# Two-layer transformer on one core: SyncE loads slot numbers four at a time, and GpSimd's sums between sends are left out

## The chip, the cores and the metric

The kernel runs on one core of one Trainium2 chip. The metric is the time of one execution on the device in microseconds (us). A core has five engines with instruction streams of their own: TensorE (PE in the profile; its weight loads are PEld), VectorE (DVE), ScalarE (ACT), GpSimd (POOL) and SyncE (SP, its queue SPq). They meet only through semaphores. In this kernel SyncE computes nothing: it waits, reads small numbers into registers and issues direct DMAs. GpSimd issues the indirect ones, and does elementwise work.

## The reference, cut to what matters

Eight batches of 512 tokens with 128 features go through two layers. Each layer adds an attention and then a mixture of experts to the tokens:

```
x = x + attention0(layernorm(x))      # 16 heads of 8, 4 key/value heads, causal
x = x + moe0(layernorm(x))            # 8 experts, the best one per token: silu(x w1a) * (x w1g) @ w2, times its probability
x = x + attention1(layernorm(x))      # latent keys and values, rotary positions, causal
x = x + moe1(layernorm(x))            # 8 experts, the best two per token: relu(x w1 + b1) @ w2 + b2, times the probabilities
```

Which expert a token goes to is known only when the gate has been computed on the chip. The change touches the two mixtures alone.

## The kernel before, in words

**Slots.** The tokens of a group of batches are sorted by expert. GpSimd scatters each tile of 128 tokens with an indirect DMA to rows of a DRAM tensor `sorted_in` (step `scatter`, line 1090), so that each block of 128 rows there holds tokens of one expert. Such a block is a slot. Layer 0 has two groups (batches 0 to 3 and 4 to 7) with 46 slots in all; layer 1 has four groups (batches 0 to 3; 4 and 5; 6; 7) with 78 slots. In the three last groups of layer 1, which share a half (a group is then called streaming), the rows of a slot lie at a place that is known only at run time.

**What is done for a slot of layer 1.** SyncE fetches the first weights of its expert into a ring of six buffers (`fetch_w1`, lines 913 to 933, 322 KB), and its rows, four slots per step (`fetch`, lines 945 to 967). TensorE turns the rows (`turn_rows`, L1299), multiplies by the first weights (`first`, L1317, 8 matmuls a slot) and by the second (`second`, L1327, 8 matmuls). ScalarE does the relu between them (L1476). VectorE adds the bias out of the ring's buffer (`second`, L1507, `w<-psum,w_now`), once a slot; with it the ring's buffer and the psum bank are free again. GpSimd then sends the 128 rows back to their tokens' places with an indirect DMA (`send`, L1098). At the end SyncE takes each half back (`take_back`, L988), VectorE adds it to X with the gates (L1541), and SyncE stores X.

**Numbers in registers.** The expert of a slot is a whole number in the table `expert_of`, the place of a streaming slot's rows one in `tile_at`. For each slot SyncE reads the number into a register with `value_load` (L916 for the expert, L962 for the place).
**The order.** Every engine's order of steps is written out by hand as a string of letters (`ORDERS`, one letter a step, from which `Plan.read_orders` makes the steps). Each engine follows its string strictly, so a step that waits holds up all that stands behind it on its engine. On SyncE, in the streaming groups, one `fetch` step (B) alternates with some three or four `fetch_w1` steps (D). `fetch_w1` waits, after its load, until VectorE or TensorE has freed the ring's buffer.

**Pauses.** `read_orders` marks a scatter, a combine (layer 0's gather back, L1108) or a send as one with a pause when two such steps stand directly before it (`MOST_IN_A_ROW` = 2). Before such a step GpSimd adds four columns of constants (`pause`, lines 1019 to 1023, `route_small<-consts`), with a wait for the pause before. By the order string there are 62 pauses: 20 before scatters, 2 before combines and 40 before sends.

Of the kernel before, what the change touches and what calls it, by code (L numbers as in the profile page):

```python
# [20 lines left out]
EXPERTS = 8  # L21
# [116 lines left out]
REGION_TILES = REGION // P  # L138
# [141 lines left out]
XT_KINDS = ("turn", "turn_ctx")  # L280
INDIRECT = ("scatter", "combine", "send")
MOST_IN_A_ROW = 2

def slot_before(layer, g, x, n):
# [109 lines left out]
class Plan:  # L395
# [53 lines left out]
    def read_orders(self):  # L449

        number = dict.fromkeys(SORTED, 0)
        for engine, letters in ORDERS.items():
            queues = {}
            for s in self.steps:
                if (s.kind not in SORTED or apart(s)) and takes_part(s, engine):
                    queues.setdefault(LETTERS[s.kind], []).append(s)
                elif SORTED.get(s.kind) == engine and takes_part(s, engine):
                    queues.setdefault(LETTERS[variant(s)], []).append(s)
            for kind, first_on in SORTED.items():
                if engine != first_on and kind != "add":  # L460
                    queues[LETTERS[kind]] = [s for s in self.orders[first_on] if s.kind == kind and takes_part(s, engine)]
            queues = {letter: iter(steps) for letter, steps in queues.items()}
            in_a_row = 0
            for letter in letters:
                s = next(queues[letter])
                self.orders[engine].append(s)
                if SORTED.get(s.kind) == engine:
                    s.n = number[s.kind]
                    number[s.kind] += 1
                if s.kind in XT_KINDS and engine == "pe":  # L470
                    n = len(self.users["xt"])
                    s.slot, s.turn = n % 3, n // 3
                    self.users["xt"].append(s)
                if s.kind == "stats" and engine == "dve":
                    s.slot = s.n % 2
                if engine == "pool":
                    s.pause = s.kind in INDIRECT and in_a_row == MOST_IN_A_ROW
                    in_a_row = (1 if s.pause else in_a_row + 1) if s.kind in INDIRECT else 0

    def take_banks(self):  # L480
# [42 lines left out]
def two_layers(nc, d):  # L523
    with ExitStack() as ctx:
# [278 lines left out]
        def _(sp):  # L803
            def load_batch(b):
                sp.dma_start(X[:, QT * b:QT * b + QT, :], d["x"].rearrange("b (t p) d -> b p t d", p=P)[b]).then_inc(x_loaded[b], DMA)

            load_batch(0)
            sp.dma_start(consts[:, :], d["consts"]).then_inc(consts_loaded, DMA)
            sp.dma_start(scratch[:, 0:MASK_COLS], d["masks"]).then_inc(consts_loaded, DMA)
# [18 lines left out]
            for s in plan.order("sp"):  # L828
# [83 lines left out]
                elif s.kind == "fetch_w1":  # L912
                    if s.x == 0:
                        sp.wait_ge(experts_known, ALL_GROUPS.index((s.layer, s.b)) + 1)
                    j = first_slot(s.layer, s.b) + s.x
                    e = sp.value_load(expert_of[half_of(s.layer, s.b)][0:1, j:j + 1], min_val=0, max_val=EXPERTS - 1)  # L916
                    if s.turn:

                        old = slot_before(s.layer, s.b, s.x, W1_RING[s.layer])
# [24 lines left out]
                elif s.kind == "fetch":  # L944
# [9 lines left out]
                    if streams(s.layer, s.b):  # L954
# [2 lines left out]
                        if s.x == 0 and is_final(s.layer, s.b):  # L957
                            sp.wait_ge(tails_set, EXPERTS * DMA)
                        tiles = sorted_in[s.layer][half_of(s.layer, s.b)].rearrange("(n p) d -> n p d", p=P)
                        for t in range(n):  # L960
                            j = first_slot(s.layer, s.b) + 4 * s.x + t
                            at = sp.value_load(tile_at[0:1, j:j + 1], min_val=0, max_val=EXPERTS * REGION_TILES + SPARE - 1)  # L962
                            sp.dma_start(rows_in[s.slot][:, t * ROW:(t + 1) * ROW],  # L963
                                         tiles[bass.ds(at, 1), :, :].rearrange("a p d -> p (a d)")).then_inc(fetched[s.slot], DMA)
                        continue
# [888 lines left out]
```

## Time and profile before

| | |
|---|---|
| runs | 1048.46, 1060.53, 1063.93 us |
| median | 1060.53 us |
| profiled execution: from its first to its last instruction (the page gives no other time of it) | 1059.9 us |
| TensorE busy, mean granted clock | 902.2 us (85%), 0.92 |
| VectorE, ScalarE, GpSimd busy | 667.9, 610.0, 534.5 us |
| moved by DMA | 141.20 MB, mean 133 GB/s |

How to read it: busy shares are averages over stages that have different limits. To about 210 us there is the attention of layer 0 alone; from there on the experts of a group run beside the attention of the batches behind it. The last attention ends near 840 us, and what is left to the end is the experts of layer 1 alone. Waiting, register and branch instructions don't count as busy, so SyncE has no busy share; its instructions are seen in the views of a line and in the chain of waits.

### The profile page before, as it was taken

To read this page: it belongs to the slowest core of one execution; us is meant where nothing else is said; L and a number is where in the kernel's file an instruction comes from. 1 tells how busy PE (TensorE), PEld (TensorE's weight loads), DVE (VectorE), ACT (ScalarE), POOL (GpSimd) and SP (SyncE) were. 2 spreads that over 40 slices of the span, in tenths; PEclk is the share of its full clock that TensorE was granted. 3 is DMA by queue.
4 is the path that set the end of the run, shared out by engine and by line. 5 is a ranking of instruction groups with operands and counts; after the bars stand their busy time and mean duration, and the time that the engine had idled before them with its cause. 6 is when DMAs were issued, how large, how long until landed. Compare 5 with 4: busy or idle time off the path is not lost.

```text
span 1059.9 us, 25406 instructions
## 1 busy us (share of the span) xinstructions
PE 902.2 (85%) x8968; PEld 600.8 (57%) x8968; DVE 667.9 (63%) x1379; ACT 610.0 (58%) x1173; POOL 534.5 (50%) x809
## 2 busy tenths in 40 slices
PE   4699999879998999889998999978998776399791
PEld 2344554436995445349974454534447766388781
DVE  1889897857457888855669987997861351011116
ACT  3168897825445786734346867856784343155541
POOL 3144454562015776752137855676865633744442
PEclk9999999879999899789999989998988888699996
DMA  5635523353755253519844273345023445357577
GB/s 145 138 85 161 152 70 88 83 162 108 216 170 125 92 144 86 128 43 302 234 133 81 84 160 93 95 116 149 28 61 90 143 133 152 99 164 217 164 211 226
DMA packets 137317, 141.20 MB, mean 133 GB/s; under 512 B 35564, under 2 KB 113452, under 8 KB 137100
## 3 DMA queue, kind: packets, MB, share of 16 engines
q1 hardware_dynamic: 130604, 126.04, 43.7%
q0 software_dynamic: 6592, 13.55, 4.1%
q8 instruction: 76, 1.25, 0.5%
q14 instruction: 45, 0.37, 0.1%
HBM read 98.73 MB, written 44.36 MB: 135 GB/s over the span
## 4 chain that ended last, share of the span: by engine, by line
PE 30%; DVE 6%; another core or an unknown queue 5%; issue 5%; SPq 4%; ACT 3%; DMA 2%; POOL 0%; DVEq 0%; ACTq 0%; POOLq 0%
PE psum L1317 8%; PE psum L1327 7%; PE psum L1248 4%; DVE neg_max L1510 2%; PE psum L1204 2%; PE psum L1230 2%; SPq L963 1%; ACT scratch L1439 1%; SPq L962 1%; PE psum L1210 1%; PE psum L1274 1%; SPq L933 1%; SPq L916 1%; PE psum L1283 1%
## 5 line engine op out<-in xcount | busy, mean ns | idle before, releaser
L1510 DVE TENSOR_REDUCE neg_max<-psum 128x2 f32<-128x768 f32 (+3 forms) x352 | 380.7, 1120 | 73.2 <-PE psum L1210 52.2
L1439 ACT ACTIVATE scratch<-psum 128x1024 f32<-128x1024 f32 x320 | 316.7, 1024 | 97.2 <-PE psum L1230 84.3
L1079 POOL TENSOR_SCALAR_AFFINE_SELECT scratch<-scratch 128x512 f32<-128x512 f32 x256 | 159.0, 642 | 150.8 <-ACT scratch L1439 149.6
L1317 PE MATMUL psum<-rows_t,w_now 128*128 128x128 f32 x1360 | 177.6, 284 | 5.3 <-issue 2.2
L1248 PE MATMUL psum<-scratch,values 128*32 128x512 f32 (+3 forms) x2048 | 173.4, 460 | 1.3 <-POOL scratch L1079 0.3
L1317 PEld LDWEIGHTS psum<-rows_t,w_now 128*128 128x128 f32 x1360 | 165.6, 198 | 13.8 <-issue 8.8
L1327 PE MATMUL psum<-w,hidden_t 128*128 x992 | 140.7, 292 | 36.4 <-ACT hidden_t L1476 15.5
L1204 PE MATMUL psum<-k_stack,q_stack 52*128 52x128 bf16 (+3 forms) x1024 | 136.2, 326 | 25.7 <-DVE neg_max L1510 10.2
L1476 ACT ACTIVATE hidden_t<-psum,w_now 128x128 f32<-128x128 f32 x312 | 88.7, 372 | 115.0 <-remote 39.6
L1327 PEld LDWEIGHTS psum<-w,hidden_t 128*128 128x128 f32 x992 | 128.0, 204 | 43.4 <-issue 43.2
L1230 PE MATMUL psum<-q_stack,k_stack 55*128 55x512 bf16 (+3 forms) x1024 | 124.9, 316 | 14.5 <-DVE neg_max L1510 5.6
L1090 POOL DMA_INDIRECT sorted_in<-xn_half,rows_of x96 | 94.4, 984 | 50.7 <-DVE xn_half L1532 28.2
L1507 DVE TENSOR_TENSOR w<-psum,w_now 128x128 f32<-128x128 f32 x78 | 22.6, 291 | 154.5 <-PE psum L1327 94.6
L1098 POOL DMA_INDIRECT returned<-w,goes_to x78 | 76.8, 984 | 81.0 <-DVE w L1507 50.7
L1204 PEld LDWEIGHTS psum<-k_stack,q_stack 52*128 52x128 bf16 x1024 | 44.0, 98 | 107.2 <-issue 45.4
L1210 PE MATMUL psum<-masks_bf 64*128 64x64 bf16 (+2 forms) x1408 | 94.6, 213 | 2.0 <-issue 2.0
L1248 PEld LDWEIGHTS psum<-scratch,values 128*32 128x32 f32 x2048 | 55.6, 112 | 65.1 <-issue 44.7
L1210 PEld LDWEIGHTS psum<-masks_bf 64*128 64x128 bf16 x1408 | 71.9, 102 | 34.1 <-issue 8.8
L1230 PEld LDWEIGHTS psum<-q_stack,k_stack 55*128 55x128 bf16 x1024 | 37.0, 96 | 75.8 <-issue 36.1
L1764 DVE SCALAR_TENSOR_TENSOR hidden_t<-w,psum 128x512 f32<-128x512 f32 x46 | 31.6, 687 | 59.1 <-PE psum L1327 33.8
L1061 POOL TENSOR_TENSOR rot<-rot 128x512 f32<-128x512 f32 x16 | 20.4, 1273 | 54.6 <-DVE rot L1507 54.5
L1069 POOL TENSOR_TENSOR max_parts<-max_rest,max_parts 32x128 bf16<-32x128 f32 x32 | 13.6, 424 | 59.7 <-ACT max_parts L1335 59.4
(141 smaller groups left out, 1027.5 us busy)
## 6 DMA issues: line engine op xcount, KB each, us to landing
w_now<-in_w SPq DMA_DIRECT2D x78, 322.0 KB
w_now<-in_w SPq DMA_DIRECT2D x46, 512.0 KB
q_stack<-q_parts SPq DMA_DIRECT2D x64, 192.0 KB
q_parts<-q_parts SPq DMA_DIRECT2D x16, 384.0 KB, 3.2
k_stack<-k_parts SPq DMA_DIRECT2D x32, 192.0 KB
q_parts<-q_parts SPq DMA_DIRECT2D x16, 256.0 KB, 3.0
w<-in_w SPq DMA_DIRECT2D x16, 256.0 KB, 4.5
scratch<-returned SPq DMA_DIRECT2D x16, 256.0 KB, 3.6
```

What stands on the lines that cost most here:

```text
L1079: pool.affine_select(out=diag, in_=diag, compare_op=ALU.is_ge, fill=0.0, base=0, pattern=[[0, 4], [1, P]], channel_multiplier=-1).then_inc ...
L1090: pool.indirect_dma_start(sorted_in[s.layer][half_of(s.layer, g)][:, :], bass.IndirectOffsetOnAxis(ap=row_of(s.layer, g, t, k), axis=0), x ...
L1098: pool.indirect_dma_start(returned[h][:, :], bass.IndirectOffsetOnAxis(ap=goes_to[h][:, j:j + 1], axis=0), kept[slot], None).then_inc(sent ...
L1204: pe.matmul(out[:, j * width:(j + 1) * width], q_stack[i][rows, pair, t * P:(t + 1) * P], k_stack[i][rows, k_of(layer, pair), 0:width], st ...
L1210: ins = pe.matmul(blocks, ident_of[half, :], mask[half, :].unsqueeze(1).to_broadcast([P // 2, n, P // 2]), start=False, stop=(first > widt ...
L1230: ins = pe.matmul(bank[u.bank + k][:, off:off + SEQ - j * P], k_stack[i][rows, k_of(layer, pair), j * P:(j + 1) * P], q_stack[i][rows, pai ...
L1248: ins = pe.matmul(bank[u.bank][CW * c:CW * c + CW, j * P:SEQ], values[batch_of(s) % 3][:, j, col:col + CW], p[:, c % 2, off:off + SEQ - j ...
L1317: ins = pe.matmul(bank[v.bank][:, c * P:(c + 1) * P], w1_now[layer][w.slot][:, n * FFN + c * P:n * FFN + (c + 1) * P], rows)
L1327: ins = pe.matmul(bank[u.bank][:, 0:P], hidden_t[h.slot][:, k * P:(k + 1) * P], w2[layer][:, bass.ds(e, 1), k * DIM:(k + 1) * DIM].rearran ...
L1439: act.activation(expd[s.slot], psum[:, u.bank:u.bank + 2, :], ACT.Exp, scale=SCALE).then_inc(read[u.bank], 1)
L1476: ins = act.activation(hidden_t[s.slot][:, c * P:(c + 1) * P], bank[u.bank][:, c * P:(c + 1) * P], ACT.Relu, bias=w[:, FFN + c:FFN + c + 1])
L1510: return dve.tensor_reduce(out=out, in_=in_, axis=AX, op=op, negate=negate)
```

## The change

SyncE reads the numbers of up to four slots at once with `values_at`, without the comparison of bounds: `fetch_w1` does so at each fourth slot of a group and takes one number from the list at each step; `fetch` reads its up to four places before it issues its up to four DMAs. TensorE's loads (L1309) and those of the tails (L941) stay as they are. In `read_orders` a send gets no pause any more. A send still counts as a step in a row, and `>=` stands for `==`, so that a scatter behind two or more sends gets one: by the order string 23 pauses are left, 21 before scatters and 2 before combines.

```diff
+LOADED = 4
...
                 if engine == "pool":
-                    s.pause = s.kind in INDIRECT and in_a_row == MOST_IN_A_ROW
+                    s.pause = s.kind in INDIRECT and s.kind != "send" and in_a_row >= MOST_IN_A_ROW
                     in_a_row = (1 if s.pause else in_a_row + 1) if s.kind in INDIRECT else 0
...
+            def values_at(table, first, n, high):
+
+                found = nc.values_load_multi_w_load_instructions(
+                    table[0:1, first:first + n], engines=[mybir.EngineType.SP], min_val=0, max_val=high,
+                    skip_runtime_bounds_check_because="the table is made on the chip of counts that cannot leave these bounds")
+                return list(found[1])
...
                 elif s.kind == "fetch_w1":
                     if s.x == 0:
                         sp.wait_ge(experts_known, ALL_GROUPS.index((s.layer, s.b)) + 1)
-                    j = first_slot(s.layer, s.b) + s.x
-                    e = sp.value_load(expert_of[half_of(s.layer, s.b)][0:1, j:j + 1], min_val=0, max_val=EXPERTS - 1)
+                    if s.x % LOADED == 0:
+                        experts = values_at(expert_of[half_of(s.layer, s.b)], first_slot(s.layer, s.b) + s.x,
+                                            min(LOADED, SLOTS[s.layer][s.b] - s.x), EXPERTS - 1)
+                    e = experts.pop(0)
...
-                        for t in range(n):
-                            j = first_slot(s.layer, s.b) + 4 * s.x + t
-                            at = sp.value_load(tile_at[0:1, j:j + 1], min_val=0, max_val=EXPERTS * REGION_TILES + SPARE - 1)
+                        found = values_at(tile_at, first_slot(s.layer, s.b) + 4 * s.x, n, EXPERTS * REGION_TILES + SPARE - 1)
+                        for t, at in enumerate(found):
                             sp.dma_start(rows_in[s.slot][:, t * ROW:(t + 1) * ROW],
                                          tiles[bass.ds(at, 1), :, :].rearrange("a p d -> p (a d)")).then_inc(fetched[s.slot], DMA)
```

## Rows read from the trace of the kernel before

**Rows 1.** The page: busy time by engine; the chain that ended last, by engine.
```profile
PE 902.2 (85%) x8968; PEld 600.8 (57%) x8968; DVE 667.9 (63%) x1379; ACT 610.0 (58%) x1173; POOL 534.5 (50%) x809
...
PE 30%; DVE 6%; another core or an unknown queue 5%; issue 5%; SPq 4%; ACT 3%; DMA 2%; POOL 0%; DVEq 0%; ACTq 0%; POOLq 0%
```

**Rows 2.** The chain of waits from 944 to 1006 us: shares by line.
```profile
by line: issue 24.8%; SPq L963 20.5%; SPq L962 18.3%; SPq L933 15.0%; SPq L916 14.7%; DMA w_now<-in_w 5.9%; DMA rows_in<-sorted_in 2.9%; SPq L928 0.6%; SPq L953 0.1%; SPq L956 0.1%; SPq L958 0.0%
```

**Rows 3.** Busy by stretch: us, PE, PEld, DVE, ACT, POOL, clock, DMA, GB/s.
```profile
944.00:1006.00 62.00, 54.70 (x435) 50.06 (x434) 7.68 (x31) 33.44 (x114) 28.26 (x39) 1.00 0.64 185
1006.00:1035.00 29.00, 25.92 (x205) 25.07 (x206) 4.12 (x15) 14.09 (x49) 13.03 (x18) 0.94 0.72 211
```

**Rows 4.** Timeline of VectorE: start, us, line, operation, [idle before]; three bias additions.
```profile
945.15 0.29 DVE L1507 TENSOR_TENSOR w<-psum,w_now 128x128 f32<-128x128 f32 x1 [1.49 <-PE psum L1327]
...
1007.86 0.29 DVE L1507 TENSOR_TENSOR w<-psum,w_now 128x128 f32<-128x128 f32 x1
...
1039.22 0.29 DVE L1507 TENSOR_TENSOR w<-psum,w_now 128x128 f32<-128x128 f32 x1 [0.67 <-PE psum L1327]
```

**Rows 5.** Groups by line, 944 to 1006, then 1007.8 to 1039.3: bias additions.
```profile
L1507 DVE TENSOR_TENSOR w<-psum,w_now 128x128 f32<-128x128 f32 x25 | 7.1, 291 | 28.1 <-PE psum L1327 23.8 <-issue 4.3
...
L1507 DVE TENSOR_TENSOR w<-psum,w_now 128x128 f32<-128x128 f32 x16 | 4.7, 292 | 24.2 <-PE psum L1327 16.8 <-issue 7.5
```

**Rows 6.** SyncE's waits (total, times, longest): 944 to 1006; 1007.8 to 1039.3; whole kernel.
```profile
SPq L928 <- DMA w_now<-in_w: 1.7, 2, 1.3
...
SPq L933 <- DVE w L1507: 5.5, 4, 2.2
...
SPq L933 <- PE psum L1317: 33.6, 27, 3.2
```

**Rows 7.** Loads of line 962, 944 to 1006: count, ns min/median/max.
```profile
L962 SPq TENSOR_LOAD <-tile_at x28: 3/268/422, 944.3 to 1005.2; - x28
```

**Rows 8.** The chain from 1004 to 1006: start, us, what; one place and its DMA.
```profile
1004.11 0.27 SPq L962
...
1004.41 0.15 SPq L962
...
1004.68 0.04 SPq L963
...
1004.83 0.34 SPq L963
...
1005.21 0.28 SPq L962
```

**Rows 9.** Timeline of GpSimd, 904 to 924: sends, and a pause (L1023).
```profile
904.98 1.00 POOL L1098 DMA_INDIRECT returned<-w,goes_to  x1 [0.16 <-issue]
906.28 0.96 POOL L1098 DMA_INDIRECT returned<-w,goes_to  x1 [0.30 <-issue]
907.27 0.21 POOL L1023 TENSOR_TENSOR route_small<-consts 128x4 f32<-128x4 f32 x1
907.64 1.00 POOL L1098 DMA_INDIRECT returned<-w,goes_to  x1 [0.16 <-issue]
...
922.26 0.96 POOL L1098 DMA_INDIRECT returned<-w,goes_to  x1 [0.30 <-issue]
```

**Rows 10.** The whole kernel's pauses (L1023): count, ns min/median/max, first and last.
```profile
L1023 POOL TENSOR_TENSOR route_small<-consts x62: 207/208/224, 219.6 to 1039.4; 128x4 f32<-128x4 f32 x62
```

**Rows 11.** The chain of waits, 900 to 926: its pieces with no releaser found.
```profile
906.50 6.72 another core or an unknown queue
913.26 12.02 another core or an unknown queue
```

**Rows 12.** Timeline, 913 to 926: VectorE, TensorE and ScalarE around the longest piece.
```profile
913.25 0.29 DVE L1507 TENSOR_TENSOR w<-psum,w_now 128x128 f32<-128x128 f32 x1 [12.55 <-remote]
...
913.78 2.07 PE L1327 MATMUL psum<-w,hidden_t 128*128 x8 [8.51 <-DVE w L1507]
...
925.30 0.89 ACT L1476 ACTIVATE hidden_t<-psum,w_now 128x128 f32<-128x128 f32 x3 [18.80 <-remote]
```

## The prediction, made before the changed kernel ran

> **What bounds the kernel now.** I read the page first. TensorE is busy for 85% of the span and leads the chain that ended last, but SyncE's queue holds 4% of that chain, with part of the 5% called issue, and another 5% has no releaser that the profile can name [rows 1]. So neither of the two engines that the change touches bounds the kernel as a whole; the question is where their 4% and 5% lie. The chain of waits in the stretch from 944 to 1006 us answers the first: the four lines of SyncE hold 20.5 + 18.3 + 15.0 + 14.7 = 68.5% of it, "issue" (here the gaps between SyncE's own instructions) 24.8%, and no matmul stands in it at all [rows 2]. For 62 us SyncE is the bound. TensorE is busy there for 54.7 of 62 us at full clock [rows 3], which looks like a bound too; but a matmul's modelled end covers gaps shorter than it, so I go by the pace instead.
>
> The pace is read off VectorE's bias additions, one a slot. From 945.15 to 1007.86 there are 25 [rows 4, 5], so 62.71 / 25 = 2.51 us a slot. From 1007.86 to 1039.22 there are 16 with both ends, so 15 steps, 31.36 / 15 = 2.09 us a slot, at a mean clock of only 0.94 [rows 3 to 5]. What differs is SyncE: in the first stretch it waits for nobody but 1.7 us for weights, in the second it waits 5.5 us for VectorE to free the ring [rows 6]. There TensorE and what hangs on it set the pace; before, SyncE did.
>
> The views of GpSimd answer the second question. While it sends indirect DMAs back to back, signals between other engines come late: between the bias addition at 913.25 and the relu at 925.30 the chain has a piece of 12.02 us without a releaser, before it one of 6.72 us [rows 11], and VectorE sat for 12.55 us, ScalarE for 18.80 us [rows 12]. Both pieces lie in a row of sends that begins at 904.98 and whose last starts at 922.26 [rows 9].
>
> **SyncE, step by step.** A streaming slot costs SyncE two numbers and two DMAs. For one place the load begins at 1004.11, the comparison at 1004.41, the address at 1004.68, the DMA at 1004.83, and the next load at 1005.21 [rows 8]. So a number with its DMA takes 1.10 us: load and gap 0.30, comparison, assertion and their gaps 0.27, address 0.15, DMA and gap 0.38. A slot takes 2.20 us of SyncE; the 2.51 measured have waits and slower issues on top, 0.31.
>
> The change removes the comparison at both: 2 x 0.27 = 0.54 us a slot. How long one load of four numbers takes no row shows. From below it is one single load, 0.268 us [rows 7]; from above four of them in a row with their gaps, 4 x 0.30 = 1.20 us. The slot then costs SyncE 2.20 - 0.54 = 1.66 us at the upper end and 1.66 - 2 x 0.30 x 3/4 = 1.21 us at the lower. I take the upper end, since only single loads are in the rows. With the 0.31 of waits it is 1.97, under 2.09 at either end: SyncE stops being the bound, and TensorE's pace is late next. The gain is 25 x (2.51 - 2.09) = 10.5 us at most. I take 9: two or three slots of it go while the ring of six fills, and the transfers get denser, as the DMA share of 0.72 against 0.64 shows at the faster pace [rows 3].
>
> The Trainium skill (Runtime: NRT & Kernel Launch, Instruction fetch mechanics) says that a bulk TENSOR_LOAD costs some 200 ns for each register. This speaks against half the change; an estimate by it is 0.8 us for four numbers, in which case the slot would cost SyncE 1.46 us with 0.31 on top, and the sum would stay, since TensorE's pace still ends it. No run so far shows such a load.
>
> A step that is moved: at a `fetch` the first row DMA leaves later, up to 1.20 + 0.15 instead of 0.57 + 0.15 us behind the step's start; its fourth starts at 1.20 + 3 x 0.53 + 0.15 = 2.94 instead of 3 x 1.10 + 0.72 = 4.02. TensorE and VectorE wait for all four, so this is a gain. The first `fetch_w1` of a group leaves up to 0.63 us later, and its second at 1.88 against 1.82, the others earlier. In six groups that is at most 6 x 0.63 = 3.8 us, and less wherever the rows are still under way; at the lower end it is a gain of 0.27 each. I take nothing.
>
> In layer 0, and where a `fetch_w1` waits for the ring, the load stands ahead of the wait and is hidden by it: SyncE waits 33.6 us in 27 pieces for TensorE there [rows 6]. If that cover went, each number would give 0.27 back. Nothing.
>
> **GpSimd, step by step.** 40 pauses go and one is added: net 39 of 62, 0.208 us each [rows 10]. In a row of sends the pause costs less than its length: from 906.28 to 907.64 with it is 1.36 us, from 904.98 to 906.28 without is 1.30 [rows 9]. That is 0.06 us for each; 8 lie in the long row, 0.5 us, which stands on the chain. Elsewhere GpSimd waits for VectorE and the pause runs in that wait. I take 0.4. What three or more indirect DMAs without a sum cost, or do to the late signals, no row shows: from above no gain over the sum's 0.06, from below no row. So it is bounded by the rivals.
>
> **Sum.** The profiled execution spans 1059.9 us, 0.6 under the median of 1060.53, in runs that spread over 15 us. 1059.9 - 9 - 0.4 = 1050.5; against the median 1051. What follows the last bias addition, 1059.9 - 1039.2 = 20.7 us, moves as it is.
>
> **Rivals.**
>
> *Another wait takes SyncE's place.* At a denser issue the weights land late, or the upper end of the load plus slow issues beside the sends keeps SyncE near 2.3 us a slot: 25 x 0.2 = 5 us or less, and where the comparison stayed in after all, 0 to 2. Around 1057. For it: SyncE already waited for weights twice in the stretch [rows 6]. Against: the later stretch holds 2.09 with 211 GB/s against 185 [rows 3].
>
> *Slower: the pause is what lets the signals through.* Place: the sends in a row from 904.98 on. Without pauses GpSimd's sequencer may run further ahead, and the signals that came in the middle of the row, such as VectorE's at 913.25, come only behind the last send. The eight matmuls at 913.78 and what they released (some 5 us of TensorE's work, [rows 12]) would then move behind 923; if the late signals of the shorter rows double as well, 6.72 + 12.02 = 18.7 us more at the worst. I price it at 16: 1059.9 - 9.4 + 16 = 1066.5. It decides from 9.4 us on, 0.24 us for each pause that is gone. For it: the late signals stand only in such rows. Against: pauses at 907.27 and each 2.7 us after did not end them [rows 9, 11].
>
> The Trainium skill (Perfetto Trace Analysis, DMA Instruction — SWDGE (GPSIMD)) bears on it: GpSimd's sequencer pushes such a DMA into a wait queue and goes on at once to the next. The trace of before can't show how far it runs; by that rule only the pause's own wait holds it back.
>
> *The pause holds the signals up.* If sums with their own semaphore are part of what makes them late, half of 18.7 us and of like pieces before it comes back, some 12: 1059.9 - 9.4 - 12 = 1038.5. For it: 8 pauses stand in the very stretch. Against: an unpaused pair is just as tight.
>
> **How the numbers follow.** Forecast 0.58, its own range 1044 to 1057; another wait 0.15 (1057); pause missing, slower 0.14 (1067); pause harmful 0.13 (1038). A measurement of this kernel can tell about 2% from no change, 21 us: under 1039 or over 1082. Under 1039 lies half of the last case and a little of the forecast, as medians of a few runs move by some us: 0.14. Over 1082 lies only the far end of the slower case: 0.04. The rest, 0.82, is within 2%. The range 1040 to 1065 leaves out about half of either outer case.
>
> **What would show it.** In the chain from some 935 us on, SyncE's lines should be gone and matmuls stand there; bias additions should follow each other by about 2.1 us; SyncE should wait for VectorE at L933 all the way. L916 and L962 should show no comparison any more, and one load for four numbers or one for each. Sends in a row should start every 1.30 us, with 23 sums left. The prediction is wrong if the pace stays over 2.3 us, or if the pieces without a releaser behind 850 us change by more than 5 us in either direction.

## The result, and the profile after

In the first comparison, 20 runs of each kernel side by side, the changed kernel took 1049.34 us (median; 1038.79 to 1054.51) and the kernel before 1057.37 us (1048.46 to 1072.52): a ratio of 0.9913, with an interval of 0.9892 to 0.9934. The forecast was 1051 us in a range of 1040 to 1065. The profiled execution spans 1047.5 us against 1059.9.

The page of the changed kernel: busy time by engine, and further down the chain that ended last, by engine; they answer to [rows 1].

```profile
PE 895.6 (86%) x8968; PEld 596.9 (57%) x8968; DVE 671.3 (64%) x1379; ACT 609.9 (58%) x1173; POOL 524.8 (50%) x770
...
PE 35%; DVE 6%; another core or an unknown queue 6%; issue 3%; ACT 2%; DMA 1%; POOL 0%; SPq 0%; DVEq 0%; ACTq 0%; POOLq 0%
```

SyncE's 4% are gone from the chain and TensorE took them. The pieces without a releaser are still there. The same is to be seen in the stretch of [rows 2]: the chain of waits of the changed kernel from 944 to 998 us, shares by line (L1326 and L1336 are the matmuls of a slot, L1317 and L1327 before).

```profile
by line: PE psum L1336 49.0%; PE psum L1326 38.7%; PE psum L1308 5.1%; issue 3.3%; DVE w L1516 1.7%; ACT hidden_t L1485 1.4%; ACT rows_t L1344 0.9%; ACTq L1483 0.0%
```

Busy time by stretch of the changed kernel, with the columns of [rows 3]: us, PE, PEld, DVE, ACT, POOL, clock, DMA share, GB/s.

```profile
944.00:998.00 54.00, 51.25 (x424) 48.24 (x423) 8.02 (x32) 31.04 (x107) 24.02 (x25) 1.00 0.76 221
998.00:1027.00 29.00, 27.57 (x230) 26.32 (x230) 5.41 (x21) 16.77 (x58) 14.07 (x15) 1.00 0.72 226
```

VectorE's bias additions of the same three slots as in [rows 4], from the timeline of the changed kernel.

```profile
943.47 0.29 DVE L1516 TENSOR_TENSOR w<-psum,w_now 128x128 f32<-128x128 f32 x1 [1.50 <-PE psum L1336]
...
997.72 0.29 DVE L1516 TENSOR_TENSOR w<-psum,w_now 128x128 f32<-128x128 f32 x1 [0.49 <-PE psum L1336]
...
1026.90 0.29 DVE L1516 TENSOR_TENSOR w<-psum,w_now 128x128 f32<-128x128 f32 x1 [0.23 <-issue]
```

These three rows carry the whole account. Up to the first of them the changed kernel is 945.15 - 943.47 = 1.7 us ahead. The 25 slots after it take 54.25 us where they took 62.71, so 8.5 us, or 2.17 against 2.51 us a slot. The next 15 take 29.18 instead of 31.36, 2.2 us. What follows the last is 20.7 us before and 20.6 after. 1.7 + 8.5 + 2.2 + 0.1 = 12.4 us, the difference of the two spans.

Most of the 2.2 us is TensorE's clock. The stretch of the kernel before ends with TensorE idle for 3.10 us behind SyncE's late rows. After one more group of eight matmuls at full speed, the granted clock falls: it is 0.57 of full over the next 3.9 us, the lower of its two levels for most of them. Here are TensorE's rows there, then busy time in those 3.9 us and in all 15 slots (columns of [rows 3]):

```profile
1008.40 1.15 PE L1327 MATMUL psum<-w,hidden_t 128*128 x8 [3.10 <-DVE w L1507]
1009.72 1.76 PE L1317 MATMUL psum<-rows_t,w_now 128*128 128x128 f32 x8 [0.16 <-issue]
...
1009.72:1013.65 3.93, 3.93 (x21) 3.93 (x22) 0.46 (x2) 1.14 (x4) 1.68 (x3) 0.57 0.75 230
...
1007.86:1039.22 31.36, 29.24 (x230) 28.01 (x230) 5.68 (x22) 15.63 (x54) 16.08 (x22) 0.95 0.75 228
```

The same of the changed kernel, where TensorE had waited only 0.30 us:

```profile
998.26 1.15 PE L1336 MATMUL psum<-w,hidden_t 128*128 x8 [0.30 <-DVE w L1516]
999.58 1.13 PE L1326 MATMUL psum<-rows_t,w_now 128*128 128x128 f32 x8 [0.16 <-issue]
...
997.72:1026.90 29.18, 27.81 (x233) 26.37 (x231) 5.59 (x20) 16.89 (x59) 13.97 (x15) 1.00 0.73 228
```

In the chains of waits the matmuls of L1317, L1327 and L1299 at this place take 1.76, 1.71 and 0.63 us before and 1.13, 0.89 and 0.44 after: 1.6 of the 2.2 us. The other 0.5 us are spread over the twelve slots behind them.

SyncE's waits in the changed kernel (in total, times, longest), 944 to 998, then 998 to 1027: they answer to [rows 6].

```profile
SPq L938 <- DMA w_now<-in_w: 3.3, 2, 3.0
SPq L943 <- DVE w L1516: 3.0, 4, 1.0
...
SPq L943 <- DVE w L1516: 9.9, 6, 2.4
```

SyncE now has time to wait for VectorE in both stretches. Its loads in the changed kernel from 944 to 998 (count, ns min/median/max, first and last start), which stand in the place of [rows 7]; the first table feeds the weights, the second the rows.

```profile
L810 SPq TENSOR_LOAD <-expert_of x8: 285/872/933, 945.6 to 995.5; - x8
L810 SPq TENSOR_LOAD <-tile_at x6: 863/888/931, 950.2 to 991.1; - x6
```

Fourteen loads instead of one a number, and no comparison behind them. A load of four is 0.87 to 0.89 us in the middle, 0.22 a number, where a single one takes 0.268 and 0.30 with its gap; so little is gained by taking them together. The shortest, 0.285 us, is a load of one number: the group of batches 4 and 5 has nine slots, and 4 + 4 + 1 are loaded. The last loads of two other groups have two and three numbers and take 0.467 and 0.677 us:

```profile
L810 SPq TENSOR_LOAD <-expert_of x1: 285/285/285, 953.2 to 953.2; - x1
L810 SPq TENSOR_LOAD <-tile_at x1: 467/467/467, 998.6 to 998.6; - x1
L810 SPq TENSOR_LOAD <-expert_of x1: 677/677/677, 925.0 to 925.0; - x1
L810 SPq TENSOR_LOAD <-expert_of x3: 299/304/308, 872.1 to 897.1; - x3
```

The last line stays unexplained: these three, ahead of the stretch, are loads of four too and took 0.30 us.

GpSimd in the changed kernel: the timeline of the long row of sends, then all pauses. They answer to [rows 9] and [rows 10].

```profile
903.90 0.96 POOL L1107 DMA_INDIRECT returned<-w,goes_to  x1 [0.31 <-issue]
905.17 0.96 POOL L1107 DMA_INDIRECT returned<-w,goes_to  x1 [0.30 <-issue]
...
920.35 0.96 POOL L1107 DMA_INDIRECT returned<-w,goes_to  x1 [0.31 <-issue]
```

```profile
L1032 POOL TENSOR_TENSOR route_small<-consts x23: 207/208/221, 217.9 to 901.0; 128x4 f32<-128x4 f32 x23
```

A send follows the one before it every (920.35 - 903.90) / 13 = 1.265 us; with a pause after each pair it was (922.26 - 904.98) / 13 = 1.33 [rows 9]. The pieces without a releaser in the chain of the changed kernel from 850 to 926 us, which answer to [rows 11]:

```profile
856.43 4.40 another core or an unknown queue
...
874.88 10.90 another core or an unknown queue
899.71 8.92 another core or an unknown queue
908.94 15.23 another core or an unknown queue
```

They are about as long as before. Two of them, 8.92 + 15.23 = 24.2 us, lie in the long row, where the kernel before had 6.72 + 12.02 and one of 2.66 just ahead, 21.4.

### The profile page after: what moved, and what is told of

It is laid out like the page before. It is cut to its first block, busy times and chain, and to the rows that moved or that the text cites. A ratio compares the mean times of both kernels' runs of the same rounds, so it can differ in the third digit from the quotient of the medians.

```text
span 1047.5 us, 24922 instructions
## 1 busy us (share of the span) xinstructions
PE 895.6 (86%) x8968; PEld 596.9 (57%) x8968; DVE 671.3 (64%) x1379; ACT 609.9 (58%) x1173; POOL 524.8 (50%) x770
## 4 chain that ended last, share of the span: by engine, by line
PE 35%; DVE 6%; another core or an unknown queue 6%; issue 3%; ACT 2%; DMA 1%; POOL 0%; SPq 0%; DVEq 0%; ACTq 0%; POOLq 0%
PE psum L1326 10%; PE psum L1336 9%; PE psum L1257 5%; PE psum L1239 3%; PE psum L1213 3%; DVE neg_max L1519 2%; PE psum L1219 1%; PE psum L1283 1%; PE psum L1308 1%; ACT scratch L1448 1%; PE psum L1292 1%; PE psum L1175 1%; PE psum L1267 1%; DVE X L1550 1%
## 5 line engine op out<-in xcount | busy, mean ns | idle before, releaser
L1326 PE MATMUL psum<-rows_t,w_now 128*128 128x128 f32 x1360 | 176.6, 283 | 4.8 <-issue 3.0
L1326 PEld LDWEIGHTS psum<-rows_t,w_now 128*128 128x128 f32 x1360 | 164.9, 197 | 13.3 <-issue 11.1
L1336 PE MATMUL psum<-w,hidden_t 128*128 x992 | 138.9, 289 | 33.5 <-DVE w L1516 13.0
L1336 PEld LDWEIGHTS psum<-w,hidden_t 128*128 128x128 f32 x992 | 126.3, 202 | 40.4 <-issue 40.3
```

The costliest lines, as they stand in the source:

```text
L1326: ins = pe.matmul(bank[v.bank][:, c * P:(c + 1) * P], w1_now[layer][w.slot][:, n * FFN + c * P:n * FFN + (c + 1) * P], rows)
L1336: ins = pe.matmul(bank[u.bank][:, 0:P], hidden_t[h.slot][:, k * P:(k + 1) * P], w2[layer][:, bass.ds(e, 1), k * DIM:(k + 1) * DIM].rearran ...
```

## The experiments

Every kernel was timed in turn with the kernel before; kernels of one batch share a chip and the runs of the kernel before, and each ratio is to those. The batches ran on chips 11, 5, 2 and 13, in this order; the number of the chip of the first comparison is not on record.

**The parts taken apart.** The first batch of four holds each half of the change alone, and SyncE's half in two ways: loads without comparison, but one number each; and loads of four numbers with their comparisons.

`pause_only` has GpSimd's half: the changed rule for pauses, SyncE as before.

```diff
-                    s.pause = s.kind in INDIRECT and in_a_row == MOST_IN_A_ROW
+                    s.pause = s.kind in INDIRECT and s.kind != "send" and in_a_row >= MOST_IN_A_ROW
```

> GpSimd's part alone: no pause before a send, SyncE as before. Theory A (SyncE's shorter work gives the gain): at most 0.5 us below the kernel before plus what the faster row of sends gives back, ratio 0.998 to 1.000; bias additions between 945 and 1008 us still 2.5 us a slot. Theory B (the pauses gave the gain): ratio 0.992. Theory C (pauses let late signals through): slower, ratio over 1.003. Sends in a row start every 1.27 us instead of 1.33 under all three.

`sp_only` has SyncE's half: the changed kernel with the old rule for pauses.

```diff
-                    s.pause = s.kind in INDIRECT and s.kind != "send" and in_a_row >= MOST_IN_A_ROW
+                    s.pause = s.kind in INDIRECT and in_a_row == MOST_IN_A_ROW
```

> SyncE's part alone: four numbers a load, no comparison, pauses as before. Theory A: ratio 0.991 to 0.993, bias additions 2.1 to 2.2 us a slot in the long stretch. Theory B: ratio 0.998 to 1.000. Theory C: faster than the whole change.

`single_unchecked` is `sp_only` with one number a load, still without comparison.

```diff
-LOADED = 4
+LOADED = 1
...
-                        found = values_at(tile_at, first_slot(s.layer, s.b) + 4 * s.x, n, EXPERTS * REGION_TILES + SPARE - 1)
-                        for t, at in enumerate(found):
+                        for t in range(n):
+                            at = values_at(tile_at, first_slot(s.layer, s.b) + 4 * s.x + t, 1, EXPERTS * REGION_TILES + SPARE - 1)[0]
```

> One number a load as before, but no comparison of bounds; pauses as before. By the rows, a slot costs SyncE 1.66 us and 0.3 of waits, below TensorE's 2.1. Theory A1 (once SyncE is under TensorE's pace more is worth nothing): the same as SyncE's part alone, ratio 0.991 to 0.993. Theory A2 (the load of four matters too): half of it, ratio 0.995 to 0.997.

`bulk_checked` is `sp_only` with the comparison of each of the four numbers put back.

```diff
-                    table[0:1, first:first + n], engines=[mybir.EngineType.SP], min_val=0, max_val=high,
-                    skip_runtime_bounds_check_because="the table is made on the chip of counts that cannot leave these bounds")
+                    table[0:1, first:first + n], engines=[mybir.EngineType.SP], min_val=0, max_val=high)
```

> Four numbers a load, each still compared with its bounds; pauses as before. The load of four was 0.87 us in the streaming groups after the change, 0.22 a number against 0.30, so a slot costs SyncE 2.20 - 0.16 = 2.04 us and 0.3 of waits, 2.35 against 2.51. Theory A1: a third to a half of the gain, 25 x 0.16 = 4 us, ratio 0.996. If the load of four is what counts: ratio 0.992.

| kernel | median us | ratio | interval | the 25 slots of the profiled execution |
|---|---|---|---|---|
| before | 1057.43 | 1 | | 62.71 us [rows 4] |
| pause_only | 1055.44 | 0.9983 | 0.9954 to 1.0011 | 61.88 |
| sp_only | 1047.02 | 0.9903 | 0.9867 to 0.9939 | 54.37 |
| single_unchecked | 1047.2 | 0.9895 | 0.9860 to 0.9930 | 54.55 |
| bulk_checked | 1056.63 | 0.9991 | 0.9966 to 1.0017 | 63.11 |

The last column is the time from the bias addition at the start of the stretch to the one 25 slots later. Without comparison the kernel gains, whether it loads four numbers or one; with it it gains nothing, though it loads four. Busy time from 944 to 998 us, in the columns of [rows 3], of `sp_only`, `single_unchecked`, `bulk_checked` and `pause_only`:

```profile
944.00:998.00 54.00, 51.02 (x424) 48.20 (x424) 8.06 (x31) 30.28 (x103) 26.66 (x37) 1.00 0.75 220
```

```profile
944.00:998.00 54.00, 50.90 (x422) 47.99 (x421) 8.27 (x32) 31.14 (x107) 26.21 (x37) 1.00 0.75 215
```

```profile
944.00:998.00 54.00, 47.55 (x383) 43.93 (x382) 7.28 (x28) 28.29 (x97) 25.83 (x36) 1.00 0.62 185
```

```profile
944.00:998.00 54.00, 47.98 (x388) 44.33 (x386) 7.29 (x28) 28.28 (x95) 21.72 (x23) 1.00 0.68 197
```

The two without comparison put 424 and 422 matmuls into the same 54 us, the two with it 383 and 388. What a load of four with comparison costs is seen in `bulk_checked`'s instructions of line 810 from 944 to 1006 us (ns min/median/max):

```profile
L810 SPq FUSED_REGOPS  x53: 5/147/348, 944.6 to 1003.8; - x53
L810 SPq SEQ_ASSERT  x53: 3/18/18, 944.8 to 1003.9; - x53
L810 SPq TENSOR_LOAD <-tile_at x7: 868/951/1054, 943.7 to 1001.9; - x7
```

Each of the 53 numbers has its comparison and its assertion again, whichever load it came with. The expectation of a third to a half of the gain (a load of four saves 0.08 us a number, 4 us in 25 slots) missed: nothing came. In the chain of `bulk_checked` from 944 to 1006 us SyncE shares the time with the weights' transfers and some matmuls, where before it stood nearly alone [rows 2]:

```profile
by line: SPq L810 21.6%; DMA w_now<-in_w 19.8%; issue 19.7%; SPq L971 13.3%; SPq L942 8.4%; PE psum L1335 8.3%; PE psum L1325 8.1%; DMA rows_in<-sorted_in 3.0%; DVE w L1515 0.5%; SPq L937 0.2%; SPq L962 0.1%; SPq L967 0.0%; SPq L965 0.0%
```

So what SyncE saves in its loads did not reach TensorE: waits for transfers took its place in the chain. Why they do, no run took apart.

The last 15 slots divide the five kernels in the same way. They take 31.31 us in `bulk_checked` and 30.70 in `pause_only`, at a mean granted clock of 0.95 and 0.94, and 29.50 in `sp_only` and 29.66 in `single_unchecked`, at 1.00. TensorE sat idle for 2.41 and 3.01 us ahead of the dip in the first two, and for 0.30 and 0.32 us at this place in the others.

**The late signals.** The next four ask what the pieces without a releaser hang on. `sends_moved` leaves the changed kernel's instructions as they are and only moves letters in GpSimd's written order: eleven sends of layer 1's first group (8) go in between the last two portions of scatters, three into the sixes and eight more into the sevens, so that the one long row is split and the sends keep up with the slots.

```diff
-        "ppp4pb44p44bp4m44pp4ppp44m44ppppppp55pppbpp55558855558b5888858855888558866666666777787777888888888888888888888888999999999++++++++"
+        "ppp4pb44p44bp4m44pp4ppp44m44ppppppp55pppbpp55558855558b5888858855888558866668886666777788888888877778888888888888999999999++++++++"
```

> The whole change, and GpSimd's order altered at one place: of the sends that stood in one row behind the last scatters of layer 1, three go ahead of four scatters that wait till 873 us, and eight more ahead of the four that wait till 898 us. Theory L (signals between engines come late as long as GpSimd issues indirect DMAs back to back): the row from 899 to 921 us shrinks to some 9 us, the bias addition of slot 29 comes near 910 us instead of 924, some 10 us are won, ratio to the kernel before 0.980 to 0.986. Rival (the late signals come from something else at that place, or only move): within 0.3% of the whole change, 0.989 to 0.993.

It took 1038.17 us, 0.9802 (0.9742 to 0.9862), as expected if the row is what counts (0.980 to 0.986). Its chain has these pieces without a releaser from 850 to 926 us:

```profile
872.43 13.22 another core or an unknown queue
897.44 4.30 another core or an unknown queue
902.91 3.83 another core or an unknown queue
```

That is 21.4 us, where the changed kernel has 4.40 + 10.90 + 8.92 + 15.23 = 39.5. The work is the same; so the pieces go with the length and the place of GpSimd's row. The changed kernel itself wasn't timed on this chip; `no_pause`, below, stands in for it.

`no_pause` takes the last 23 pauses out too.

```diff
-                    s.pause = s.kind in INDIRECT and s.kind != "send" and in_a_row >= MOST_IN_A_ROW
+                    s.pause = False
```

> SyncE as in the whole change, and no pause before any indirect DMA, scatters and combines included. If pauses neither free nor hold signals: as the whole change, ratio 0.989 to 0.993. If a pause lets late signals through: the rows of scatters from 797 to 884 us hold them longer, ratio over 0.995. If it holds them up: under 0.987.

It took 1050.63 us, 0.9932 (0.9892 to 0.9973), which can't be told from the changed kernel. A pause of one sum, in scatters or sends, gives and costs nothing that can be measured here.

`five_sums` is `sp_only` with five sums in place of one.

```diff
-                if s.pause:
+                for _ in range(5 if s.pause else 0):
```

> SyncE's part alone, and each of the 62 pauses made of five sums, each waiting for the one before, some 1.5 us instead of 0.2. In a row two sends then take some 4.1 us instead of 2.66. If a gap without indirect DMAs lets late signals through: bias additions come within the rows, and the kernel is not slower than SyncE's part alone (0.990) or faster. If it is only the length of the row that counts: the row of 14 sends grows by some 10 us, ratio 1.000 or more.

It took 1023.47 us, 0.9685 (0.9631 to 0.9739): 32 us under the kernel before, with 248 more sums. SyncE's half, which is in it, gave 0.9903 in the batch before; about two thirds of the gain are thus the gaps'. Its chain, by engine, has no share left for the unknown releaser:

```profile
PE 28%; POOL 9%; issue 6%; DVE 5%; DMA 2%; ACT 2%; SPq 2%; another core or an unknown queue 0%; POOLq 0%; DVEq 0%; ACTq 0%
```

In its place stands GpSimd with 9%. Its timeline shows why: a pair of sends with its sums takes 884.75 - 880.63 = 4.12 us, and the last one starts at 1001.81, 28.6 us behind the last bias addition.

```profile
880.63 1.00 POOL L1107 DMA_INDIRECT returned<-w,goes_to  x1 [0.49 <-issue]
881.94 0.96 POOL L1107 DMA_INDIRECT returned<-w,goes_to  x1 [0.30 <-issue]
882.93 1.32 POOL L1032 TENSOR_TENSOR route_small<-consts 128x4 f32<-128x4 f32 x5
884.75 1.00 POOL L1107 DMA_INDIRECT returned<-w,goes_to  x1 [0.50 <-issue]
...
1001.81 1.00 POOL L1107 DMA_INDIRECT returned<-w,goes_to  x1 [0.49 <-issue]
```

`lean` follows the comparison to where it is left: TensorE's load of each slot's expert, and SyncE's load of the regions' ends, in the changed kernel.

```diff
-                        at = sp.value_load(ends_at[0:1, e:e + 1], min_val=e * REGION, max_val=(e + 1) * REGION - P)
+                        if e % LOADED == 0:
+                            ends = values_at(ends_at, e, LOADED, EXPERTS * REGION - P)
+                        at = ends.pop(0)
...
-                    reg[layer, b, s.x] = pe.value_load(expert_of[half_of(layer, b)][0:1, j:j + 1], min_val=0, max_val=EXPERTS - 1)
+                    reg[layer, b, s.x] = nc.values_load_multi_w_load_instructions(
+                        expert_of[half_of(layer, b)][0:1, j:j + 1], engines=[mybir.EngineType.PE], min_val=0, max_val=EXPERTS - 1,
+                        skip_runtime_bounds_check_because="the table is made on the chip of counts that cannot leave these bounds")[1][0]
```

> The whole change, and the comparison left out of TensorE's 124 loads and the eight of the tails, the latter four at a load. In the stretch where TensorE sets the pace its loads run ahead of the matmuls, hidden. Expected as the whole change, ratio 0.989 to 0.993; if the loads stand between the matmuls, up to 0.2 us a slot less from slot 37 on, 8 us, ratio 0.984.

It took 1039.13 us, 0.9835 (0.9774 to 0.9895), the second of the two cases expected (0.984, the loads stand between the matmuls). Its bias additions show a gain in the pace, where TensorE is the bound: 52.7 us for the 25 slots against 54.25, and the 15 after them in 1016.32 - 988.37 = 27.95 us, 1.86 a slot against 1.95, both at a granted clock of 1.00. `no_pause`, on the same chip, took 54.99 and 29.59 us. But these 2.8 us are the smaller part of the 10.5 by which the profiled span is under that of the changed kernel. The other 7.8 lie ahead of the stretch. The pieces without a releaser are shorter there too (29.2 us behind 850 us against 39.5), and how much of the 7.8 is the comparison's wasn't separated.

```profile
988.37 0.29 DVE L1520 TENSOR_TENSOR w<-psum,w_now 128x128 f32<-128x128 f32 x1 [0.35 <-PE psum L1340]
...
1016.32 0.28 DVE L1520 TENSOR_TENSOR w<-psum,w_now 128x128 f32<-128x128 f32 x1
```

**How long a gap, and where.** Three kernels try to keep what the gaps gave and lose the backlog of sends. `three_sums` is `sp_only` with three sums; `five_then_none` has five up to the 16th send of layer 1 and none behind it; `five_then_two` has two there and `lean`'s loads.

```diff
+                    s.pause = 3 if s.kind in INDIRECT and in_a_row == MOST_IN_A_ROW else 0
...
+                    s.pause = 5 if s.kind in INDIRECT and in_a_row >= MOST_IN_A_ROW and (s.kind != "send" or s.n < 16) else 0
...
+                    s.pause = (5 if s.kind != "send" or s.n < 16 else 2) if s.kind in INDIRECT and in_a_row == MOST_IN_A_ROW else 0
```

> As five_sums, with three sums of GpSimd where that kernel does five (before every third of indirect DMAs in a row, in every row); SyncE's side as in the change. Five sums gave 0.9685 of before, and its last send starts 28.6 us after the last bias addition, where one sum gives 0.9903. Theory A (a gap in the row lets late signals through, and the effect grows with the gap): three sums take some 0.9 us between pairs of DMAs, a pair then 3.5 us against 4.1, so the backlog of sends is gone or nearly so (62 sends x 0.3 = 19 us less of the 28), and part of the late signals come back: ratio 0.955 to 0.975. Theory B (a threshold: what helps is that the wait queue in front of GpSimd runs empty, which needs all of the 1.3 us): three sums are as one, the pieces of late signals of 10, 9 and 15 us stand in the chain again, ratio 0.985 to 0.99.

> As five_sums up to the 16th send of layer 1, and no sum at all between the 62 sends after it. Five_sums has its last bias addition at 973.2 us and its end at 1021.8, since sends at 4.1 us a pair lag behind TensorE. Without sums a send takes 1.27 us, so 46 us of backlog at the 16th send are caught up after some 55 sends at TensorE's 2.1 us a slot (62 x 0.8 = 50 us), and the tail of 48.6 us falls to 20.6. Theory A (any row of indirect DMAs without a gap delays signals): from 872 us on sends stand back to back for some 40 us, and pieces of late signals stand there, 10 to 18 us in sum: span 1004 to 1012, ratio 0.953 to 0.96. Theory B (only rows with a wait for another engine in them, or the rows of scatters and combines, matter): no such piece, the slots keep their 2.1 us, span 994, ratio 0.942.

> Up to the 16th send five sums as in five_sums, from there two sums after each pair of sends; beside it TensorE's loads of numbers and SyncE's load of the regions' ends are without comparison, as in lean. Two sums make a pair of sends 3.1 to 3.2 us, 1.6 a send against TensorE's 1.86 to 2.1 us a slot, so 46 us of backlog shrink by some 25 to 30, and GpSimd ends some 5 to 15 us behind. Theory A (the effect grows with the gap): late signals in the last row cost some 5 us; with lean's 8 us of gain the span is 995 to 1008, ratio 0.945 to 0.955. Theory B (two sums are as none in the last row): 10 to 18 us of late signals there, span 1008 to 1018, ratio 0.955 to 0.965.

| kernel | median us | ratio | interval |
|---|---|---|---|
| before, on this chip | 972.7 | 1 | |
| three_sums | 977.94 | 1.0058 | 1.0030 to 1.0086 |
| five_then_none | 979.64 | 1.0079 | 1.0051 to 1.0107 |
| five_then_two | 987.27 | 1.0150 | 1.0118 to 1.0182 |

Every expectation missed, because the batch fell on a chip on which the kernel before itself takes 972.7 us, where 1055 to 1057 had been measured on the others. None of the three has a piece without a releaser. `five_then_none` has none even in its row of 36 bare sends from 858.5 us on, so on this chip it is not the gap that keeps them away, and each gap is a loss. The loss is larger than the ratios, since all three have SyncE's half of the change in them, which gains. How much three sums would give on a chip with late signals stays open.

**The changed kernel once more.** `after_again` is the changed kernel without an edit. It ran on one more chip, on which the kernel before takes 975.01 us.

> The changed kernel itself once more, beside the kernel before. The kernel before took 1055 to 1057 us on the chips of the first batches and 972.7 us on the chip of the last one, where three kernels with gaps between the indirect DMAs took 978 to 987 us and had no piece without a releaser in their chains. Theory A (the late signals are a property of the chip and not only of the kernel; where they are absent, rows of indirect DMAs cost nothing and gaps only cost time): if the kernel before takes some 973 us here, the changed kernel's chain shows no piece called another core, and the removed comparisons give their 0.8 to 1.2% alone: ratio 0.985 to 0.992, some 962 us. Theory B (that chip is faster for another reason, such as its clock or its transfers, and the late signals are there too): the pieces of some 10, 9 and 15 us stand in the chain again, at the same places. If the kernel before takes some 1056 us here, both expect the first result again: 0.989 to 0.993, with those pieces.

It took 962.37 us (958.49 to 965.17), 0.9867 (0.9835 to 0.9899), within what was expected if nothing comes late here (0.985 to 0.992). So the gain of the change doesn't hang on the late signals. Its chain, by engine, has no unknown releaser:

```profile
PE 34%; DVE 8%; issue 3%; SPq 3%; DMA 2%; ACT 1%; POOL 0%; DVEq 0%; ACTq 0%; POOLq 0%
```

Here the same instructions were profiled on two chips, so their traces can be laid side by side. VectorE's instructions stand within 0.5 us of each other up to 210 us. Then GpSimd's first row of scatters runs to 229.9 us on both, each DMA at the same time to 0.06 us. ScalarE's first instruction behind 218 us in it, on the first chip (timeline: start, us, line, [idle before]):

```profile
229.94 0.60 ACT L1344 ACTIVATE ctx_raw<-psum 128x512 f32<-128x512 f32 x1 [12.47 <-remote]
```

and on the last:

```profile
220.20 0.60 ACT L1344 ACTIVATE ctx_raw<-psum 128x512 f32<-128x512 f32 x1 [2.75 <-PE psum L1257]
```

On the first it starts at the very moment at which the last scatter ends, although TensorE had made its input 10 us earlier. TensorE is slowed as well: its matmuls of line 1159 come one every 0.7 us on the first chip, idle before each for what the view calls issue, and eight in 0.43 us on the last. On the first:

```profile
222.06 0.27 PE L1159 MATMUL psum<-xn_t,wkv 128*32 128x128 f32 x1 [0.51 <-issue]
222.78 0.32 PE L1159 MATMUL psum<-xn_t,wkv 128*32 128x128 f32 x2 [0.45 <-issue]
223.49 0.27 PE L1159 MATMUL psum<-xn_t,wkv 128*32 128x128 f32 x1 [0.40 <-issue]
```

and on the last:

```profile
220.73 0.43 PE L1159 MATMUL psum<-xn_t,wkv 128*32 128x128 f32 x8
```

In `five_sums`, on a chip with late signals, the same ScalarE instruction came between the two:

```profile
222.28 0.60 ACT L1344 ACTIVATE ctx_raw<-psum 128x512 f32<-128x512 f32 x1 [4.71 <-remote]
```

The first such row leaves the first chip 11.3 us behind, and the distance grows in steps to 1047.5 - 959.1 = 88.4 us at the end; the 25 slots of the stretch themselves differ by only 54.25 - 51.15 = 3.1.

## Why the prediction was right, point by point

**SyncE bound the stretch, and the comparison was its price.** Right. The term was 9 us for 25 slots; 8.5 came. The pace is 2.17 us a slot against 2.09 forecast and 2.51 before, and the chain has TensorE alone in it. `single_unchecked` takes out the comparisons alone and has the whole gain; `bulk_checked` keeps them and has none. That the load of four with its comparisons gained nothing at all, instead of a part, was not foreseen and is open.

**The load of four was bounded by 0.268 and 1.20 us, and 1.20 was taken.** It takes 0.87 to 0.89 in this stretch, inside the bounds. The Trainium skill (Runtime: NRT & Kernel Launch, Instruction fetch mechanics) has some 200 ns for each register of a bulk load (from HBM; the tables here lie on the chip), by which an estimate for four is 0.8 us; the trace agrees in the stretch, with 0.22 a number, and not in the loads of four ahead of it, with 0.30 us in all. Since TensorE's pace ended the sum at either bound, the choice cost nothing. It also means that half of SyncE's edit is idle: `single_unchecked` is as fast.

**The gain stops at TensorE's pace.** Right, but the forecast took the last 15 slots as unchanged, and they gave 2.2 us more. SyncE is in the chain of these slots neither before nor after; 1.6 of the 2.2 us are the low clock at their start, which had followed TensorE's idle time of 3.10 us. The forecast had the sign of it in hand, a mean clock of 0.94 [rows 3], and took 2.09 us a slot as TensorE's pace all the same; at a clock of 1.00 it is 1.95. This is the term that was left out. Together with 1.7 us before the stretch it makes the profiled difference 12.4 and not 9.4.

**How near the number came is in part luck.** 1051 was forecast and 1049.34 came, but the 1060.53 it was counted from was the median of three runs; that of the 20 is 1057.37. The medians differ by 8.0 us, where 9.4 was the sum and 12.4 the profiled difference. The profiled difference compares one execution of each kernel, and the 20 executions of a kernel spread over 24 us before and 16 us after.

**The sums of GpSimd are worth 0.4 us.** Right as far as can be seen: `pause_only` has an interval of 0.9954 to 1.0011, and `sp_only` without that half is as fast as the whole. Sends were to come every 1.30 us and come every 1.265. The 23 sums left are as forecast.

**The rivals.** That another wait takes SyncE's place fell with the pace. That the pause lets the signals through, or holds them up, fell both: the pieces in and just ahead of the long row went from 21.4 to 24.2 us, those behind 850 us from 36.8 to 39.5 (under the 5 us that were to prove the prediction wrong), `pause_only` and `no_pause` moved nothing. The reasons given against these two were the ones that held, but the mechanism behind them was not known. It is now in part: in three of the five batches a row of indirect DMAs goes with late signals. There one sum of 0.2 us is too short a gap to matter, and five sums, 1.5 to 1.85 us from the end of a DMA to the next start, free nearly all of them. Forecasting a gap's effect from a sum's length alone would have missed this, and so would have the run of one kernel on one chip.

**What stays open.** Why the signals are late on some chips and not on others no run shows, nor that it is the chip: the batches with late signals ran first and the two without last, and of the four chips on record none was used twice, so a change that came with time is not ruled out. The number of packets is not what differs: both traces move the same ones, with 76 and 42 packets of instructions in both, and GpSimd's own DMAs take the same time. Whether the delay sits in the delivery of a semaphore or in the engines' own supply of instructions, at which TensorE's 0.7 us from matmul to matmul points, wasn't separated. The kernel before was not profiled on the last two chips, so its 82 us less there are taken from its times alone.

## What to carry to other kernels

Where an engine that issues DMAs bounds a stretch, price each instruction between its DMAs, and check the pace against the slowest consumer: here the comparison behind a load cost 0.27 us a number and its removal was the whole gain, while loading four numbers at once added nothing that could be measured. Look at the clock of the stretch from which a pace is taken: if it is below 1.00, the pace holds the idle time of the stretch ahead of it. A gain in a queue ends at the next engine's pace, so ask which engine has the same comparison left, as TensorE had here (`lean`, 0.9835). When signals come late beside a row of indirect DMAs, compare one and the same kernel on more than one chip before spending work on it. The gaps of `five_sums` gained some 2% beyond SyncE's half on one. Their milder forms made kernels with that same half 0.6 to 1.5% slower than the kernel before on another.

## What the runs showed of the hardware

- The same program takes 1049.34 us on one chip and 962.37 us on another, with VectorE's instructions within 0.5 us of each other up to 210 us, just ahead of the first row of indirect DMAs.
- In three of the five batches pieces without a releaser stand beside rows of indirect DMAs. There VectorE sat idle for 15.25 us (`after`) and ScalarE for 18.80 us [rows 12], and TensorE's matmuls came 0.7 us apart (`after`). In the first row of `after` the wait ended with the row's last DMA (229.94 us); in the long one 2.9 us behind it (924.20 against 921.31). On chips 2 and 13 rows of 36 and 33 such DMAs left no piece without a releaser in the chain.
- SyncE's loads of one, two, three and four numbers take 0.285, 0.467, 0.677 and 0.87 us, but some of four ahead of the stretch 0.30; a single load in the kernel before takes 0.268 [rows 7]. The comparison and its assertion cost 0.27 us a number and are issued for each number, also behind a load of four.
- The granted clock of TensorE fell to 0.57 for 3.9 us after it had sat idle for 3.10 us and run one group of eight matmuls. In `pause_only`, after 3.01 us, the first group was slow already (2.07 us for eight); in `after`, after 0.30 us, the clock stayed at 1.00.
- Indirect DMAs follow each other every 1.265 us on GpSimd where nothing stands between them, the same on both kinds of chip.
- Without the comparison behind TensorE's own load, a slot takes 1.86 us in the last stretch (`lean`) instead of 1.95 (`after`) or 1.97 (`no_pause`, on the chip of `lean`).
